# A graph network kernel: the two convolutions wait for their gathers seven at a time instead of eight

## The reference, cut to what matters

```python
def gcn_conv(x, W, b, src, dst, n_nodes):
    h = x @ W
    ones = jnp.ones(src.shape[0], dtype=h.dtype)
    deg = jax.ops.segment_sum(ones, dst, num_segments=n_nodes) + 1.0
    dinv = jax.lax.rsqrt(deg)
    norm = dinv[src] * dinv[dst]
    msg = h[src] * norm[:, None]
    agg = jax.ops.segment_sum(msg, dst, num_segments=n_nodes)
    agg = agg + h * (dinv * dinv)[:, None]
    return agg + b
h1 = jax.nn.relu(gcn_conv(embedding, W1, b1, src, dst, n))
h2 = jax.nn.relu(gcn_conv(h1, W2, b2, src, dst, n))
```

## Time and profile before

| | us |
|---|---|
| median of 3 runs | 5349.65 (5347.81 to 5350.41) |
| span of the profiled execution | 5935.3 |
| first convolution in the profile, 2878 to 4088 | 1210 |
| second convolution in the profile, 4088 to 5262 | 1174 |
| GpSimd busy with L1857, both convolutions | 1483.7 |
| TensorE busy in both convolutions | 1113.9 |

### The profile page before, as it was taken

How to read it: one execution, slowest core, us unless ns; L and a number is a source line. 1 busy time by engine, 2 the same in 40 slices (tenths; PEclk the granted TensorE clock), 3 DMA queues, 4 the chain that set the end, 5 groups by cost and what they waited for, 6 DMA issues and landing times. The chain is left out here.

```text
span 5935.3 us, 66919 instructions
## 1 busy us (share of the span) xinstructions
PE 3546.3 (60%) x13782; PEld 2710.2 (46%) x13783; DVE 2982.8 (50%) x6982; ACT 1018.9 (17%) x2146; POOL 3055.9 (51%) x2888
## 2 busy tenths in 40 slices
PE   4744455454389865998444544454445454466998
PEld 3633233232267654776433433333434444455666
DVE  5466566666899964445433333334333333354443
ACT  0111121121179801221000000000000000013121
POOL 1266677676368624221466666663666666612111
PEclk9877767776599976998566566655555555566999
DMA  4487666666578762223311111111111111123221
GB/s 108 136 217 211 202 207 203 204 206 195 158 227 271 224 188 88 63 63 97 106 28 28 29 28 28 29 29 32 28 29 28 28 29 28 29 62 98 70 87 37
DMA packets 432122, 617.01 MB, mean 104 GB/s; under 512 B 100329, under 2 KB 309161, under 8 KB 431721
## 3 DMA queue, kind: packets, MB, share of 16 engines
q1 hardware_dynamic: 304733, 389.03, 21.1%
q0 software_dynamic: 107440, 200.97, 14.1%
q10 hardware_dynamic: 19852, 25.94, 1.6%
HBM read 419.67 MB, written 209.64 MB: 106 GB/s over the span
## 5 line engine op out<-in xcount | busy, mean ns | idle before, releaser
L1857 POOL DMA_INDIRECT big<-t_d,src_tiles x1564 | 1483.7, 949 | 957.2 <-issue 450.8
L2080 PE MATMUL v_bank<-big,v_oh 128*128 x3328 | 716.2, 390 | 1216.6 <-issue 830.3
L2080 PEld LDWEIGHTS v_bank<-big,v_oh 128*128 128x128 f32 x3328 | 674.7, 300 | 1302.8 <-issue 1302.2
L653 POOL DMA_INDIRECT big<-xl_d,src_steps x832 | 859.8, 1033 | 378.1 <-issue 356.0
L1935 DVE TENSOR_TENSOR big<-big,v_bank 128x64 f32 x1664 | 366.5, 220 | 1285.3 <-DMA xj_d<-big 973.2
L759 PE MATMUL se_z_ps<-big,se_oht 128*128 x1664 | 608.7, 517 | 628.5 <-issue 385.9
L759 PEld LDWEIGHTS se_z_ps<-big,se_oht 128*128 128x128 f32 x1664 | 386.8, 250 | 850.4 <-issue 780.7
L692 DVE TENSOR_TENSOR se_z<-se_z_ps,big 128x528 f32<-128x528 f32 x416 | 291.4, 700 | 461.1 <-DMA es_ts<-src_p 256.8
L1122 PE MATMUL ae_bank<-ae_v,ae_oh 128*128 128x266 f32 x1664 | 402.3, 397 | 49.8 <-DVE big L1106 36.7
L1081 POOL TENSOR_TENSOR ae_v<-ae_v,ex 128x1792 f32<-128x1792 f32 x104 | 334.1, 3215 | 178.1 <-DMA ae_v<-xj_d 178.0
L1122 PEld LDWEIGHTS ae_bank<-ae_v,ae_oh 128*128 128x128 f32 x1664 | 310.4, 191 | 141.5 <-DVE big L1106 53.0
(11 more groups left out here) (468 smaller groups left out, 5316.9 us busy)
## 6 DMA issues: line engine op xcount, KB each, us to landing
xj_d<-big SPq DMA_DIRECT2D x208, 528.0 KB
ae_v<-xj_d SPq DMA_DIRECT2D x208, 528.0 KB
se_dlb<-dlr_d SPq DMA_DIRECT2D x104, 256.0 KB
big<-t_d,src_tiles POOLq DMA_INDIRECT x1564
buf_d<-ne_blank SPq DMA_DIRECT2D x4, 4112.0 KB
e_xs<-buf_d SPq DMA_DIRECT2D x106, 129.0 KB, 2.1
big<-xl_d,src_steps POOLq DMA_INDIRECT x832
cp_y<-y_d SPq DMA_DIRECT2D x14, 896.0 KB, 7.4
```

Source lines behind the costliest of these rows:

```text
L653: nc.gpsimd.indirect_dma_start(half_of(u)[:, k, :], None, table, bass.IndirectOffsetOnAxis(ap=m.src[:, t:t + 1], axis=0)).then_inc(landed[ ...
L1857: nc.gpsimd.indirect_dma_start(rows[:, t % RING, :], None, table, bass.IndirectOffsetOnAxis(ap=m.srct[:, t:t + 1], axis=0)).then_inc(lande ...
L2080: last = nc.tensor.matmul(bank[u][:, k * MH:(k + 1) * MH], oh[:, u, k, :], of_block(rows, at[k]), start=True, stop=True)
```

## The change

GpSimd's part of `convolve` is rewritten; nothing else is. A gather that is the eighth of its group now adds to a semaphore of its own, `last_in`, and the first seven to `landed`. Ahead of group g GpSimd waits until seven gathers of group g - 1 have landed, that is of the group that it has issued just before. After four gathers of group g it waits for the eighth of group g - 1 and adds 1 to `tiles_in`. After the last gather it waits for the last group and adds 1.

```diff
-                    if g >= 2:
-                        pool.wait_ge(landed[g % 2], 16 * GS * (g // 2))
-                        pool.sem_inc(s["tiles_in"], 1)
+                    if g >= 1:
+                        pool.wait_ge(landed[(g - 1) % 2], 16 * (GS - 1) * ((g + 1) // 2))
                     if g + NB // GS + 2 > RING // GS:
                         pool.wait_ge(s["summed"], g + NB // GS + 2 - RING // GS)
                     for t in range(g * GS, min((g + 1) * GS, NT)):
+                        k = t - g * GS
+                        if g >= 1 and k == GS // 2:
+                            pool.wait_ge(last_in[(g - 1) % 2], 16 * ((g + 1) // 2))
+                            pool.sem_inc(s["tiles_in"], 1)
                         nc.gpsimd.indirect_dma_start(rows[:, t % RING, :], None, table,
-                                                     bass.IndirectOffsetOnAxis(ap=m.srct[:, t:t + 1], axis=0)).then_inc(landed[g % 2], 16)
-                for g in (TG - 2, TG - 1):
-                    pool.wait_ge(landed[g % 2], 16 * (GS * (g // 2) + min(GS, NT - g * GS)))
-                    pool.sem_inc(s["tiles_in"], 1)
+                                                     bass.IndirectOffsetOnAxis(ap=m.srct[:, t:t + 1], axis=0))\
+                            .then_inc(landed[g % 2] if k < GS - 1 else last_in[g % 2], 16)
+                pool.wait_ge(landed[(TG - 1) % 2], 16 * ((GS - 1) * ((TG - 1) // 2) + NT - (TG - 1) * GS))
+                pool.sem_inc(s["tiles_in"], 1)
```

More of the change, by code:

```diff
@@ L1819, in convolve @@
         bank = [ctx.enter_context(nc.psum_tensor(f"v{which}_bank{i}", [P, 512], F32)) for i in range(8)]
-        s = {n: m.sem(f"v{which}_" + n) for n in "in0 in1 tiles_in oh_ready summed added started xt_in weights".split()}
-        landed = [s["in0"], s["in1"]]
+        s = {n: m.sem(f"v{which}_" + n) for n in "in0 in1 last0 last1 tiles_in oh_ready summed added started xt_in weights".split()}
+        landed, last_in = [s["in0"], s["in1"]], [s["last0"], s["last1"]]
         iota = bank[3 + which][:, 0:P]
```

## The result

| | median, us | ratio to before | 95% interval |
|---|---|---|---|
| kernel before (5 runs) | 5350.41 (5347.81 to 5357.35) | | |
| changed kernel (5 runs) | 5373.52 (5367.98 to 5379.42) | 1.0037 | 1.0024 to 1.0049 |

The change makes the kernel slower, by 0.0037 x 5350 = 20 us (23 us between the medians; 13 to 26 by the interval). The direction was forecast and the time lies in the range. The size, 41 us, was not met: about half of it came.

A forecast was written before the change was run, and what follows sets the result against it. GpSimd's gathers, one per 1.25 us, were taken to bound the convolutions. Telling and mid-group wait 0, wait ahead 41 us: 5349.65 + 41 = 5391 us; its own range 5370 to 5428, 8 in 10 from 5345 to 5428.

The forecast's parts named there:

- GpSimd sets the pace in the timed runs: In both convolutions: unrecorded, gathers follow every 1.25 us, so 782 gathers take at least 976 us in each.
- TensorE's pace: Rival: TensorE bounds the convolutions in timed runs too, lost time comes out of GpSimd's stops, 5350 us; chance 0.16.
- The split of the missing time: Of 585.7 us the profile exceeds timed runs, 388 lie in the convolutions, up to 122 in the other gathering stage.
- something that comes with recording: Claim that something with gathers under recording slows the other engines, making the profiled execution 585.7 us longer than timed runs.
- The queue runs at least seven gathers ahead: GpSimd's queue is ahead of its gathers, so TensorE learns of a group 2.4 to 2.5 us after its last gather began.
- telling term: Telling TensorE after four gathers of the next group gains nothing, since it is already told at the landing: 0 us.
- T: Start of a group's eighth gather; the next group's first was forecast to move from T + 1.25 to T + 1.42 to T + 1.46.
- mid-group wait: Wait for the eighth gather after four of the next group: holds up no gather, 5.0 us of work queued; 0 us.
- The rival that the telling matters: In the convolutions TensorE is told four gathers, 5 us, earlier once in each: 10 us faster, 5340; chance 0.09.
- The wait ahead: Ahead of each group, waiting for seven gathers delays the first gather 0.21 us at 194 places: 41 us; bounds 0 and 56.
- The wait's rival: Unrecorded landings are seen at 2.24 us or less, so the wait ahead of a group costs nothing: 5350; chance 0.17.
- The pauses: GpSimd's unexplained idle of about 2 us at 14 places in the convolutions; the change might expose 22 us more, upper bound only.

The follow-up runs named there:

- second recording: The kernel before, unedited, profiled once more: span 5357.8 us against 5935.3 in the first profile; ratio 0.9999.
- experiment 3: Kernel before, but TensorE told after four gathers of the next group; one semaphore for all eight, no wait for seven; ratio 1.0004.
- experiment 2: Changed kernel's wait for seven gathers alone, with TensorE told at the head of a group as in the kernel before; ratio 1.0041 to the kernel before, 5377.07 us.
- experiment 11: Kernel before, waits and telling unmoved, but a group's first seven gathers counted on `landed` and its last on `last_in`; ratio 0.9965.
- experiment 5: Kernel before, but ahead of each group GpSimd waits for all eight gathers of the group just issued and tells TensorE there; ratio 1.0714.

## Why the prediction was right and wrong

**GpSimd sets the pace in the timed runs** (an inference; its rival, TensorE's pace, had 0.16): right. The second recording shows TensorE waiting 858.1 us for GpSimd's telling. The split of the missing time, 388 us in the convolutions and 122 in the other gathering stage, was measured as 382 and 147. The cause that was named, something that comes with recording, is not borne out: the other thirteen recordings of this study have none of it. What slowed that one execution is open.

**The queue runs at least seven gathers ahead, telling term 0**: right. After the change TensorE is told at T + 2.4, a median of 2.43 to 2.48, as before, except at every 13th group; experiment 3 gives 1.0004. The mid-group wait costs 0, as said. The rival that the telling matters falls.

**The wait ahead, 0.21 us x 194 = 41 us**: right, measured 39.4 in the changed kernel and 42.7 in experiment 2, of which 1.1 stand in the kernel before too (median T + 1.42 in the first and T + 1.45 in the second convolution, against T + 1.42 to T + 1.46). That it is so close is in part luck. By its own terms, T - 1.25 + 2.43 to 2.47 + 0.22, the gather begins at T + 1.40 to T + 1.44, which is 0.15 to 0.19 us late and 29 to 37 us in all, and a landing of 2.53 gives 0.25 us and 49, not 0.29 and 56. The forecast added 0.02 us that no row has. The term that was too small is the 0.20 us from a passed wait to the gather: in the changed kernel a gather starts 0.26 us (median) after the last landing signal that it waits for. The wait's rival, that landings are seen earlier unrecorded, falls with experiment 11: about 39 us in the timed runs too. The figure of the Trainium skill, "DMA: Bandwidth & Descriptors", section "Anatomy of one DMA — SWDGE (gpsimd) path", an estimate of 2.08 us for this gather, would have made the term 0. The trace agrees for the packets, whose last ends about 2.1 us after the start (median 2.08 in the changed kernel, 2.11 in the second recording of before), and disagrees for the wait, which passes at 2.43 to 2.48; it was right to go by the row of the wait.

**The pauses**: here the prediction failed. The step reads that before "up to eight queued gathers hide part of such a pause, now four to eight", and puts "as much again", 22 us, at the upper end of the bounds. The size (22.3 us of pauses) was right by accident: it stood for 14 gaps of 1.6 us, and there are 12 of 1.8. The sign was wrong, and the forecast itself took 0. The pauses were taken for a property of the queue that the change could only expose more. They hang on how the gathers are counted, and the change counts them on four semaphores in the place of two: 22.3 us of pauses shrink to 3.6. So 41 - 19 = 22 us would have been the sum with that term, and 20 to 23 were measured. The rows to suspect this were there, but nothing in them tells that a semaphore has to do with it; only the experiments do. What I could have done was to leave room below as well, since I did not know the cause of what I bounded: of the edit's three parts (the wait ahead, the telling, the two new semaphores) the third got no term at all.

**The profile of the changed kernel**: the idle of about 0.5 us ahead of groups came as said (0.51, and 0.39 at some), and inside groups it is 0.30 but for the small pauses. The forecast that its span would stay within 30 us of 5935.3 was wrong: 5371.8. I had taken the disturbance for a part of every recording. That belongs to the same habit, to treat a feature of one recording as constant.

**Experiments**: my price for the wait for all eight (1.045 to 1.050) was too low against 1.0714, since I let the gather start 0.20 us after the wait passes, where behind an instruction that also tells another engine it is 0.75, and took the pauses for gone.

## What to carry over

Look at every object an edit adds, not only at its waits: here counting on two more semaphores brought some 0.4%, and the wait they were added for cost 0.7%. The best versions need no wait ahead at all: the kernel before with its groups counted on three or four semaphores in turn (0.9961, 0.9954) is as fast as any of the others without pauses (0.9949 to 0.9965; their intervals overlap). When a profile's span is 11% over the timed runs, record the same kernel again before pricing anything in it, and let an unexplained pause have a bound on both sides.

## What the runs showed of the hardware

- Indirect gathers of 128 rows (32 KB) leave GpSimd one every 1.249 us, 0.944 of it recorded as busy. The last packet of one ends about 2.1 us after its start, a wait on its full count passes at 2.43 to 2.48 us.
- A gather that itself waits starts 0.26 us after the last landing signal that it waits for (changed kernel, median); one behind an instruction that waits and then tells another engine starts 0.75 us after that instruction (experiment 5).
- With two semaphores counting the gathers, a pause of some 1.8 us comes every 112 gathers, at which the kernel before tells TensorE 4.2 to 4.7 us late (T + 6.7 to T + 7.2); with three or four it is gone, or 0.24 us every 104 gathers where GpSimd waits for seven. The cause is open.
- One of two recordings of the same kernel was 577 us longer, all of it in stages where GpSimd issues indirect DMAs (147, 43, 382 and 6 us), but not in every such stage: two others, L1599 and L2526, took the same time in both.
